# First layer's linear attention: the keys' context gathered in three fp32r passes, with a new order of work on all engines

## The reference

```python
qh = softmax(Wq q, over the head's 64 rows) * 64**-0.5     # q = layernorm(x)
kh = softmax(Wk k, over the 1024 columns)                  # k = v = context
context = einsum('bhdn,bhen->bhde', kh, vh)
out = einsum('bhde,bhdn->bhen', context, qh)
out = Wo out + bo;  out = out / norm(out) * g * sqrt(128)
x = x + tanh(g_xattn[0]) * out
```

## Time and profile before

| | us |
|---|---|
| median of 3 executions | 3104.53 |
| profiled execution, its own time | 3103.07 |
| its span, first to last instruction | 3101.2 |
| PE busy in the span | 3014.5 (97%) |
| DVE / ACT / POOL busy | 2034.2 / 1234.9 / 1922.8 |
| mean granted TensorE clock | 0.985 |
| first layer (360 to 1225), PE busy | 831.3 of 865 |

### The profile page before, as it was taken

The page is one execution under the profiler, slowest core; times in us unless marked ns, Lnnn a source line. Parts: engine busy times, 40 slices in busy tenths (PEclk is TensorE's granted clock), DMA queues, the critical chain, the costliest instruction groups (busy, mean ns, idle before and its releaser), DMA issues.

```text
span 3101.2 us, 41067 instructions
## 1 busy us (share of the span) xinstructions
PE 3014.5 (97%) x14547; PEld 2463.1 (79%) x14547; DVE 2034.2 (66%) x2509; ACT 1234.9 (40%) x1898; POOL 1922.8 (62%) x1344
## 2 busy tenths in 40 slices
PE   8999889999999998899999999999999999999899
PEld 7888758787878777688888888888888888887687
DVE  4232457777777764576767676767777676767685
ACT  3111255555555552333433434343434343434332
POOL 4231465554555553687877777777777787878344
PEclk9999989999999999899999999999999999999899
DMA  8333511212121214422245222253232542223321
GB/s 225 109 124 114 186 40 41 72 53 79 45 82 42 82 35 143 149 109 95 108 133 175 105 102 101 101 176 136 101 114 96 175 151 107 108 95 114 131 89 55
DMA packets 188127, 333.34 MB, mean 107 GB/s; under 512 B 10592, under 2 KB 103136, under 8 KB 185952
## 3 DMA queue, kind: packets, MB, share of 16 engines
q1 hardware_dynamic: 188000, 331.67, 31.2%
HBM read 256.14 MB, written 75.50 MB: 107 GB/s over the span
## 4 chain that ended last, share of the span: by engine, by line
PE 55%; DVE 1%; issue 1%; POOL 1%; ACT 0%; DMA 0%; SPq 0%; DVEq 0%; ACTq 0%; POOLq 0%
PE pair L1971 22%; PE pair L1910 22%; PE pair L1951 3%; PE pair L1936 3%; PE pair L2452 2%; PE pair L1945 2%; PE pair L2411 1%; DVE f_rt L2337 0%; DMA f_w_raw<-in_L_signT 0%; PE pair L2403 0%; DVE f_y L2361 0%; DVE f_xs L2351 0%; ACT f_xs_hi L2273 0%; POOL f_xs_lo L2211 0%; DVE f_rt L2341 0%
## 5 line engine op out<-in xcount | busy, mean ns | idle before, releaser
L1873 DVE RECIPROCAL g_rsum<-pair 128x512 f32<-128x512 f32 x128 | 429.2, 3353 | 36.4 <-PE pair L1945 25.4
L1910 PE MATMUL pair<-g_xn_hi,g_wq_hi 128*128 128x512 f32 x1024 | 400.7, 391 | 3.0 <-POOL g_wq_lo L1612 2.1
L1910 PE MATMUL pair<-g_xn_lo,g_wq_hi 128*128 128x512 f32 x1024 | 399.9, 391 | 0.0
L1910 PE MATMUL pair<-g_xn_hi,g_wq_lo 128*128 128x512 f32 x1024 | 399.9, 391 | 0.0
L1971 PE MATMUL pair<-g_wo_hi,g_at_hi 128*128 128x512 f32 x992 | 385.9, 389 | 0.0
L1971 PE MATMUL pair<-g_wo_lo,g_at_hi 128*128 128x512 f32 x992 | 385.9, 389 | 0.0
L1971 PE MATMUL pair<-g_wo_hi,g_at_lo 128*128 128x512 f32 x992 | 385.9, 389 | 0.0
L1859 DVE SCALAR_TENSOR_TENSOR g_res<-pair,g_tg,g_res 128x512 f32<-128x512 f32 x256 | 191.3, 747 | 266.0 <-PE pair L1971 263.4
L1612 POOL TENSOR_TENSOR g_wq_lo<-g_wq_raw,g_wq_hi 128x1024 fp32r<-128x1024 f32 x129 | 310.6, 2423 | 0.6 <-ACT g_wq_hi L1749 0.6
L1749 ACT ACTIVATE g_q_hi<-g_q_raw 128x512 fp32r<-128x512 f32 x128 | 80.9, 632 | 500.0 <-POOL g_q_raw L1689 500.0
L1689 POOL TENSOR_TENSOR g_q_raw<-g_q_raw,g_rot_b 128x512 f32<-128x512 f32 x128 | 226.3, 1768 | 55.6 <-DVE g_rot_b L1841 55.6
(11 more groups left out here) (251 smaller groups left out, 7141.6 us busy)
## 6 DMA issues: line engine op xcount, KB each, us to landing
g_wq_raw<-in_L_Wq SPq DMA_DIRECT2D x64, 1024.0 KB, 7.1
g_wo_raw<-in_L_Wo SPq DMA_DIRECT2D x62, 1024.0 KB, 6.3
values_split<-c_v SPq DMA_DIRECT2D x64, 256.0 KB, 2.8
keys_split<-c_k SPq DMA_DIRECT2D x32, 512.0 KB, 2.7
xn_turned<-a_x2T SPq DMA_DIRECT2D x16, 1024.0 KB, 7.8
g_k<-keys_split SPq DMA_DIRECT2D x32, 512.0 KB, 3.3
g_v<-values_split SPq DMA_DIRECT2D x32, 512.0 KB, 7.6
c_cx_raw<-in_ctxT SPq DMA_DIRECT2D x16, 512.0 KB, 7.4
```

What stands on the lines that cost most here:

```text
L1873: V.reciprocal(rsum[:, :], p_sum[:, :]).then_inc(rsum_done, 1)
L1910: mm = M(bank[:, :], w[a][:, i, cols], x[b][:, i, :], start=(i == 0 and t == 0), stop=(i == KT - 1 and t == 2))
```

## The change

`cT` and `keT` become pairs of `hi` and `lo` tiles, and `gather` becomes three fp32r passes. New pieces: `ct_hi` (ScalarE, 128x1024 a batch), `ct_lo` (GpSimd, 128x1024 a batch) and `k_low(b, r)` (VectorE, 128x512, eight a batch), which subtracts the rounded copy from PSUM. A bank with a turned key unit is free only when `k_low` has read it. `cT_hi` lies over the tile x2n, `w2` over `g_sb`, `qs3` moves. `normal_2` waits for the gathers, `gather_out` for `outT` of the batch before. SP's order becomes `load_x`, `load_c`, `store_n(s-3)`, `load_ct`, `store_x`. All four engines' lists are in a new order.

```diff
-    cT = sb("cT", [P, KT, P])
+    cT = {"lo": sb("cT_lo", [P, KT, P], F32R), "raw": sb("cT_f", [P, KT, P], over="cT_lo")}
-    keT = [sb(f"keT{i}", [P, MT, P]) for i in range(2)]
+    keT = [{t: sb(f"keT{i}_{t}", [P, MT, P], F32R) for t in ("hi", "lo")} for i in range(2)]
...
+    cT["hi"] = sb("cT_hi", [P, KT, P], F32R, over="x2n")
...
-            bank_free[unit] = (kept[kind], b * UNITS_OF[kind] + r + 1)
+            bank_free[unit] = (keT_lo if kind == "k" else kept[kind], b * UNITS_OF[kind] + r + 1)
...
+    def ct_lo(b):
+        if exists(b):
+            pool.wait_ge(ct_hi_done, b + 1)
+            TT(cT["lo"][:, :, :], cT["raw"][:, :, :], cT["hi"][:, :, :].bitcast(F32), ALU.subtract).then_inc(ct_lo_done, 1)
...
+    def ct_hi(b):
+        if exists(b):
+            act.wait_ge(ct_land, 16 * b + 16)
+            after(act, gathered, KT * b)
+            if b == 0:
+                act.wait_ge(x_land[1], 16)
+            after(act, turned["n"], 2 * (b - 2))
+            A(cT["hi"][:, :, :], cT["raw"][:, :, :], ACT.Copy).then_inc(ct_hi_done, 1)
...
     def normal_2(b):
+            dve.wait_ge(gathered, KT * min(b + 3, BATCH))
...
+    def k_low(b, r):
+        if exists(b):
+            dve.wait_ge(kept["k"], KT * b + r + 1)
+            V.tensor_tensor(keT[r % 2]["lo"][:, :, :], blocks(bank_of["k", b, r][:, :], 4),
+                            keT[r % 2]["hi"][:, :, :].bitcast(F32), ALU.subtract).then_inc(keT_lo, 1)
...
             if r == 0:
-                pe.wait_ge(ct_land, 16 * b + 16)
-            pe.wait_ge(kept["k"], KT * b + r + 1)
-            M(p_g, cT[:, r, :], keT[r % 2][:, :, :], start=(r == 0), stop=(r == KT - 1)).then_inc(gathered, 1)
+                pe.wait_ge(ct_lo_done, b + 1)
+            pe.wait_ge(keT_lo, KT * b + r + 1)
+            for n, (a, c) in enumerate(SPLIT):
+                mm = M(p_g, cT[a][:, r, :], keT[r % 2][c][:, :, :], start=(r == 0 and n == 0),
+                       stop=(r == KT - 1 and n == 2))
+            mm.then_inc(gathered, 1)
```

More of the change, by code:

```diff
@@ L1239, in step @@
                     wb_lo(7)
-                q_norm(s, 4)
                 norm_scale(s - 1, 1)
@@ L1299, in step @@
                     wb_hi(1)
+                n_keep(s - 3, 0)
+                if s == 1:
+                    wb_hi(2)
+                q_exp(s, 2)
+                q_exp(s, 3)
                 out_keep(s - 1, 1)
                 if s == 1:
-                    wb_hi(2)
+                    wb_hi(3)
+                n_keep(s - 3, 1)
+                if s == 1:
+                    wb_hi(4)
+                ct_hi(s)
+                q_keep(s, 0)
+                q_exp(s, 4)
+                k_exp(s, 0)
+                n_round(s - 3)
+                q_keep(s, 1)
+                q_exp(s, 5)
+                k_exp(s, 1)
                 out_square(s - 1)
@@ L1328, in step @@
                     wb_hi(6)
+                xn_hi(s + 1)
+                q_keep(s, 2)
+                k_exp(s, 2)
                 q_keep(s, 3)
@@ L1352, in step @@
             def step(s):
[L1353 to L1366, removed]
@@ L1367, in step @@
-                q_shift(s, 0)
-                q_max(s, 1)
-                q_inverse(s - 1, 6)
+                k_low(s - 1, 2)
                 residual_2(s - 3)
-                moments_2(s - 3)
+                q_total(s - 1, 7)
                 q_shift(s, 1)
-                q_total(s - 1, 7)
+                k_low(s - 1, 3)
+                k_low(s - 1, 4)
                 k_inverse(s - 1)
                 residual(s - 2)
-                q_inverse(s - 1, 7)
-                moments_1(s - 2)
@@ L1378, in step @@
[L1378 to L1381, removed]
+                k_low(s - 1, 5)
+                moments_1(s - 2)
+                aggregate_1(s - 2)
+                k_low(s - 1, 6)
+                k_low(s - 1, 7)
+                normal_1(s - 2)
+                q_max(s, 2)
+                q_total(s, 0)
+                q_inverse(s - 1, 7)
+                q_shift(s, 2)
+                moments_2(s - 3)
+                w2_scale(s - 1)
@@ L1382, in step @@
+                q_max(s, 3)
                 aggregate_2(s - 3)
+                q_total(s, 1)
+                q_inverse(s, 0)
+                route_max(s - 2)
+                q_max(s, 4)
                 normal_2(s - 3)
[L1384 to L1387, removed]
                 q_inverse(s, 1)
-                w2_scale(s - 1)
-                route_max(s - 2)
+                q_shift(s, 3)
+                route(s - 2)
@@ L1391, in step @@
+                q_total(s, 2)
                 moments_x(s + 1)
[L1392 to L1398, removed]
-                q_max(s, 5)
                 q_shift(s, 4)
                 k_max(s, 0)
+                q_max(s, 5)
+                aggregate_x(s + 1)
                 q_shift(s, 5)
-                norm_total(s - 1)
+                q_total(s, 3)
@@ L1404, in step @@
+                q_inverse(s, 2)
+                k_max(s, 1)
                 q_inverse(s, 3)
                 normal_x(s + 1)
+                q_max(s, 6)
+                k_max(s, 2)
+                norm_total(s - 1)
+                q_max(s, 7)
+                q_total(s, 4)
+                norm_floor(s - 1)
+                q_shift(s, 6)
+                k_max(s, 3)
+                q_inverse(s, 4)
+                q_shift(s, 7)
+                q_total(s, 5)
+                q_max(s + 1, 0)
@@ L1406, in step @@
+                q_total(s, 6)
+                k_low(s, 0)
+                q_inverse(s, 5)
+                k_low(s, 1)
+                q_inverse(s, 6)
+                q_max(s + 1, 1)
+                q_shift(s + 1, 0)
                 if s == BATCH:
@@ L1453, in step @@
                 gather(s, 4)
+                q_project(s + 1, 2)
+                gather(s, 5)
                 k_turn(s, 7)
-                gather(s, 5)
+                q_project(s + 1, 3)
+                q_turn(s, 6)
                 gather(s, 6)
+                gather(s, 7)
                 if s == BATCH:
@@ L1460, in step @@
                 x_turn(s - 1, 0)
-                gather(s, 7)
                 x_turn(s - 1, 1)
-                q_project(s + 1, 3)
+                w2_make(s)
+                q_project(s + 1, 4)
                 q_turn(s, 7)
-                w2_make(s)
                 lora_down(s - 1)
-                q_project(s + 1, 4)
-                q_turn(s + 1, 0)
+                outT(s, 0)
                 if s == BATCH + 1:
```

152 lines of the change are left out of this document (67 added, 85 removed).

## The result

The changed kernel takes 3139.23 us (median of 4 executions, 3134.94 to 3144.28) against 3104.65 us (3104.31 to 3106.80) for the kernel before: a ratio of 1.0111 with a 95% interval of 1.0098 to 1.0125, so 35 us slower. The profiled execution took 3140.67 us, span 3138.9; against the earlier trace rows and its span of 3101.2 that is 37.7 us more (each kernel's profiled execution lies 1.5 us off its median, in opposite directions).

A forecast was written before the change was run, and what follows sets the result against it. TensorE was taken to set the pace before the change. Per step -1.5 + 0.3 + 2.5 + 0.3 + 0.5 = +2.1 us, over 14 steps +29; the forecast took 3104.5 + 27, rounded to 3131 us, range 3085 to 3150.

The forecast's parts named there:

- the likeliest case: Whole kernel: `route` held under GpSimd's block, TensorE stands at `q_project`, 3131 us (own range 3112 to 3150); chance 0.66.
- The meeting of `route` and GpSimd: VectorE's `route` waits under GpSimd's block from x_lo to `add_bias`, which ends 9.8 us after `lora_down`.
- the two walks: At `q_project(s+1,6)`, counted from `lora_down`'s end: `q_shift` lets it start after 13.7 us, TensorE gets there after 11.0.
- TensorE's own gain: TensorE's step: gathers save 1.4 us, an old wait of 0.17 goes; together -1.5 us a step.
- small waits: Turns and other units within 0.1 us of their wait, behind copy and `k_low`: 0.3 us a step (0 to 1.0).
- The extra 0.3 at `k_project(s+1,1)`: TensorE waits another 0.3 us there for `k_max(s,0)` and its exponential, behind `q_shift(s,4)`.
- The clock: TensorE's clock sometimes falls to 1.2 GHz after the stands: 0.5 us a step, between none and 2.4.
- The last step: Reckoned as one of the 14 steps s = 2 to 15, at +2.1 us.
- Filling: Start of the stage: the longer way from turn to gather costs 3 us (-2 to 8), against 2.8 gained by gathers.
- The first (3086): VectorE and GpSimd don't meet, TensorE keeps the pace: -1.2 us a step, 3086 us; chance 0.20.
- The second: Half of GpSimd's block is in `route`'s way, the stall cancels the gain: 3101 to 3108 us; chance 0.10.
- The third: The keys' bank chain of copy and `k_low` becomes the bound: +0.5 us a step, 3112 us; chance 0.04.

The follow-up runs named there:

- E1: The changed kernel with `add_bias(s-2)` moved behind `q_norm(s,4)` on GpSimd; 3103.08 us, ratio 0.9999 to the kernel before.
- e2: As e1, and on VectorE `q_shift(s,4)` and `k_max(s,0)` put ahead of `q_total(s,2)` and `moments_x(s+1)`; 3098.90 us, ratio 0.9985 to the kernel before.
- e5: The changed kernel with `gather` as one fp32 call on the hi parts, remainders still made; 3159.68 us, ratio 1.0181 to the kernel before.
- e7: e2 with the last four `wb_lo` of step 1 moved behind `q_norm(s,6)` on GpSimd; 3092.65 us, ratio 0.9962 to the kernel before.
- E8: e7 with `add_bias(s-2)` back at its early place, behind `q_norm(s,1)`, from s = 16 on; 3090.35 us, ratio 0.9952 to the kernel before.
- e9: e2 with each `k_low` done twice on VectorE; 3146.67 us, ratio 1.0143 to the kernel before.
- e3: The changed kernel with `route(s-2)` moved behind `k_max(s,0)` on VectorE, GpSimd's list untouched; 3108.82 us, ratio 1.0021 to the kernel before.

## Why the prediction was right, point by point

**Direction and mechanism: right.** 3131 was forecast for 3139, and the likeliest case is the one that happened. E1 shows it as cause: the time goes with `add_bias`'s place alone.

**The meeting of `route` and GpSimd: right, almost to the tenth.** GpSimd's block was reckoned at 9.05 us and 0.5 for the hold of `normal_2`; it runs from 842.76 to 852.24, 9.48. VectorE is held once each by c_lo, the two q_norm and `add_bias`, as said. From there to TensorE's start 1.3 + 2.65 = 3.95 was reckoned; it is 856.17 - 852.24 = 3.93. The stand was put at 2.5 (1.5 to 3.2); 35.0 / 14 is 2.5 of idle time. By the starts it is 2.7, which is what the two walks gave (13.7 - 11.0): from the turn ahead to `q_project` it is 643.40 - 640.35 = 3.05, and 635.08 - 634.72 = 0.36 in e2, which does not stand there. First the changed kernel, then e2:

```profile
640.35 0.60 PE L1062 MATMUL pair<-a_ident,a_qs 128*128 128x128 f32 x4
643.40 0.47 PE L1088 MATMUL pair<-a_wq_hi,a_xn_hi 128*128 128x512 f32 x1 [2.45 <-DVE a_qs L955]
...
645.32 0.40 PE L1174 MATMUL pair<-a_wb_hi,a_xT_lo 128*128 128x512 f32 x1
645.67 0.50 PE L1077 MATMUL pair<-a_cc_hi,a_wk_hi 128*128 128x512 f32 x1
646.01 0.40 PE L1077 MATMUL pair<-a_cc_lo,a_wk_hi 128*128 128x512 f32 x1
```
```profile
634.72 0.60 PE L1062 MATMUL pair<-a_ident,a_qs 128*128 128x128 f32 x4
635.08 0.48 PE L1088 MATMUL pair<-a_wq_hi,a_xn_hi 128*128 128x512 f32 x1
...
637.01 0.40 PE L1174 MATMUL pair<-a_wb_hi,a_xT_lo 128*128 128x512 f32 x1
637.25 0.39 PE L1077 MATMUL pair<-a_cc_hi,a_wk_hi 128*128 128x512 f32 x1
```

**TensorE's own gain: right in size.** -1.5 and +0.3 for small waits made -1.2. In e2, the stand at the first `q_project` of the step makes the distances to it and behind it 0.83 and 0.30 where 0.23 is usual, so 0.67 in all; without it the step is 50.22 - 0.67 = 49.55, and 1.3 below 50.89. The gather gives 1.2 of this (e5; 1.4 was reckoned), the old wait 0.17. The 0.3 for small waits does not show in the steady steps. So the gather was put 0.2 too high and the waits 0.3 too high, and the two errors nearly cancel.

**The extra 0.3 at `k_project(s+1,1)`: right, and hidden in the list of waits.** The waits show no stand there, but the starts do: 645.67 - 645.32 and 646.01 - 645.67 are 0.35 and 0.34 us (last lines of the first fence above), 637.25 - 637.01 is 0.24 in e2, where TensorE comes later than `q_shift` and `k_max`. So 0.2 us, in each step at full clock. It starts as was said, right behind the small read of the exponential, which ends at 645.62, here in ScalarE's timeline:

```profile
645.43 0.19 ACT L758 ACTIVATION_READ_ACCUMULATOR a_ke<-pair,a_kneg 128x1 f32 x1
```

TensorE's ends are modelled, so a wait of this size leaves no idle time in the list; e1 has the same two distances. In the steps where the clock falls, the slower matmuls cover it.

**The clock: the term that was too small.** Without it the sum was +1.6 a step; the four steps at full clock measure 52.48 - 50.91 = +1.57, and by the starts the parts are -1.3, +2.7 and +0.2. The clock was put at 0.5 a step. It falls in eight of the 12 steps and costs 1.3 us each time (53.82 on average against 52.48), 0.89 on average: 0.4 a step too little. The terms as reckoned add up to 29 us; the forecast took 27 and gives no reason for it. The profiled executions differ by 37.6. Of these 8 us, 4.4 are in the 12 steps (29.6 against 12 x 2.1), by the clock.

**The last step: mis-sized.** It was reckoned as one of the 14, +2.1; it is +5.3. That gives another 3 of the 8 us. Its stand is longer than the 2.5 us of the others, and a stretch of slow matmuls follows it (from 1178.13):

```profile
1177.06 0.47 PE L1088 MATMUL pair<-a_wq_hi,a_xn_hi 128*128 128x512 f32 x1 [3.28 <-DVE a_qs L955]
```

A fifth instruction of `route` is held here. In the lists of VectorE and GpSimd this is s = 15, with no batch s+1, so `rstd_x(s+1)` is left out of GpSimd's list and `ct_lo` comes directly behind `add_bias`; L1033, of 0.23 us elsewhere, ends at 1174.80, `ct_lo` at 1174.77:

```profile
1172.61 2.19 DVE L1033 SCALAR_TENSOR_TENSOR a_sel<-a_prio,a_sm,a_sel 128x8 f32<-128x8 f32 x1
```
```profile
1172.41 2.36 POOL L679 TENSOR_TENSOR a_cT_lo<-a_cT_f,a_cT_hi 128x1024 fp32r<-128x1024 f32 x1
```

That is 2.0 us more of hold, less the 1.2 of `moments_x(s+1)`, which is left out as well: the 0.8 by which this stand is longer. In e1, where neither `add_bias` nor `ct_lo` meets this `route`, the last step is 48.23, as in the kernel before (48.13). Two small waits for `k_low` in it (0.34 and 0.68) are in e1 too, so they are not the loss.

**Filling: right by two errors.** Start and first step are together +0.8, where -2.8 + 3 = +0.2 was reckoned. But the first `w2_make` starts 4.9 us earlier and the first step is 5.7 longer: e7 shows most of the latter to be the `wb_lo`, which block a q_norm on GpSimd, and not the longer way from turn to gather: with four of them moved, e2's first step falls from 60.17 to 54.46 (52.80 before). The sum came out near by luck.

**Rivals.** The first (3086) is the price of the same work if the meeting is avoided. E8, with the meeting avoided and both ends mended, comes to 3090; its steady step is 50.25, so -0.6 where -1.2 was reckoned. It doesn't occur in the change as made. The second needed `add_bias` out of the way; that is e1, 3103 against its 3101 to 3108. The third is refuted by e2 and its distance measured by e9.

The rule that decided the forecast holds here in both halves. The Trainium skill ("SBUF — State Buffer", section "Who interferes with whom") states it: a VectorE instruction with two SBUF inputs contends with a GpSimd instruction that reads SBUF, and one with at most one SBUF input, outside the 2-port modes, does not. The trace agrees: L1028 takes 2119 ns beside `add_bias` and 227 without; `k_low`, one input from PSUM and one from SBUF, takes 636 to 694 ns in all 128, of which some 45 run beside a GpSimd instruction. The `tensor_scalar` L1021, with one tensor input, is among the held ones: 772 ns here (median) and 231 in e3; so is L998, whose 2.07 us the prediction set against 0.23.

## What to carry to other kernels

In this kernel a tiny VectorE instruction with two SBUF inputs costs as much as is left of the GpSimd instruction that it meets (a `tensor_scalar` with one tensor input does too), and a chain of dependent ones loses one GpSimd instruction per link where GpSimd works back to back. So before reordering either engine, lay both lists side by side on a common clock and look which chain of small instructions falls under which block, then put the long GpSimd piece where VectorE is busy with PSUM operands or reductions. Look at the steps in which pieces drop out of a list as well: what moves up there can meet the chain too. A saving on the pacing engine is only had when every other engine's list still comes in time; here 1.3 us a step was earned and 2.8 lost (53.37 against e1's 50.59, means of the 12 steps) by the place of one instruction whose result nobody was waiting for.

## What the runs showed that was not expected

- A stand of about 2.5 us on TensorE is followed by the lower clock level in eight steps of 12 and not in four, with the same work around it. A fall costs another 1.3 us on top of the stand.
- The exclusion works the other way too: `cc_lo` on GpSimd, which met VectorE's `normal_2` (2.03 us), takes 2.81 instead of 2.36 us, in all 12 steady steps. In e2, e7 and e8 the first `q_project` of every steady step still has 0.44 us of idle time ahead of it; which of the held pieces that is was not tried.
- The first of three fp32r passes behind an fp32 turn takes 828.84 - 828.52 = 0.32 us to the next start, the others 0.24 and 0.23, and the turn ahead of it 0.35 instead of 0.44. The gain must be read over both: 1.29 against 1.14.
